# Layer 0 of a four-layer kernel: ScalarE takes over the output copies, and gathered rows are summed two tiles per three quads

## The reference, cut to what matters

```python
scores = softmax(flat @ router_w.T + router_bias)
topk_scores, topk_idx = top_k(scores, 4)                 # 4 experts for each row
topk_scores = topk_scores / sum(topk_scores)
h = silu(flat @ gate_w[e].T) * (flat @ up_w[e].T)        # each expert e, hidden size 128
expert_out = h @ down_w[e].T
out = sum over the 4 chosen e of topk_scores[e] * expert_out[e]
out = out + silu(flat @ sgate_w.T) * (flat @ sup_w.T) @ sdown_w.T    # shared part
```

## Time and profile before

| | us |
|---|---|
| median of the runs | 1239.35 |
| the profiled execution, its own time | 1241.5 |
| its span in the trace | 1239.7 |
| the quad loop of layer 0, first `gate_up` to last output copy | 452.6 to 669.0 |
| first instruction of the RWKV phase | 672.17 |

### The profile page before, as it was taken

The page is one execution under the profiler, slowest core; times in us unless marked ns, Lnnn a source line. Parts: engine busy times, 40 slices in busy tenths (PEclk is TensorE's granted clock), DMA queues, the critical chain, the costliest instruction groups (busy, mean ns, idle before and its releaser), DMA issues. The chain is left out here.

```text
span 1239.7 us, 19813 instructions
## 1 busy us (share of the span) xinstructions
PE 897.0 (72%) x5652; PEld 691.5 (56%) x5652; DVE 783.5 (63%) x2423; ACT 630.2 (51%) x1304; POOL 513.5 (41%) x634
## 2 busy tenths in 40 slices
PE   3796666664439999929974466677668999999910
PEld 2633555553328889929863134344457977777710
DVE  5489589998765657404777699999867411016436
ACT  4355677774833234414322566776665545555500
POOL 0003555554146666644773775000005662036055
PEclk9998777776559999969987778888777999999965
DMA  7950000000501146436543111000031132223032
GB/s 208 289 160 1 1 0 0 0 0 20 222 28 44 45 128 191 142 121 176 159 125 100 47 47 31 1 0 1 1 130 53 57 107 82 61 75 96 27 94 60
DMA packets 133844, 97.00 MB, mean 78 GB/s; under 512 B 11648, under 2 KB 125696, under 8 KB 132736
## 3 DMA queue, kind: packets, MB, share of 16 engines
q1 hardware_dynamic: 121472, 70.79, 19.1%
q0 software_dynamic: 12288, 25.19, 6.9%
HBM read 45.61 MB, written 50.33 MB: 77 GB/s over the span
## 5 line engine op out<-in xcount | busy, mean ns | idle before, releaser
L1110 POOL DMA_INDIRECT e_xs<-h_tok,rows_of x128 | 128.8, 1007 | 101.7 <-DVEq L1571 35.4
L739 ACT ACTIVATE mask<-ps_q,k_neg 128x256 bf16<-128x256 f32 x256 | 101.0, 489 | 37.3 <-PE ps_q L853 37.3
L1123 POOL DMA_INDIRECT e_got<-e_ys,e_rows_of x64 | 65.7, 1027 | 127.1 <-DMA e_ys<-e_y_rows 108.2
L1259 PE MATMUL e_ps_gu<-e_w_all,e_x_turned 128*128 x384 | 96.9, 398 | 12.8 <-DVE e_hidden L1729 12.7
L1738 DVE COPY e_y_rows<-e_ps_y 128x512 f32<-128x512 f32 x20 | 13.8, 692 | 137.9 <-PE e_ps_y L1307 137.9
L853 PE MATMUL ps_q<-q_parts,pick 128*128 (+1 forms) x256 | 59.4, 368 | 48.9 <-DVE mask L651 42.1
L1442 ACT ACTIVATE e_hidden<-e_ps_up 128x512 f32<-128x512 f32 x80 | 47.8, 597 | 84.2 <-PE e_ps_up L1289 84.2
L2226 POOL DMA_INDIRECT c_got<-e_ys,rows_of x64 | 71.2, 1112 | 36.2 <-issue 19.2
L1110 POOL DMA_INDIRECT e_xs<-h_tok,e_rows_of x64 | 65.5, 1024 | 49.4 <-DVEq L1571 17.1
L1259 PEld LDWEIGHTS e_ps_gu<-e_w_all,e_x_turned 128*128 128x128 f32 x384 | 72.5, 199 | 23.0 <-issue 14.4
L1437 ACT ACTIVATE e_hidden<-e_ps_gu 128x512 f32<-128x512 f32 x48 | 28.7, 598 | 110.4 <-PE e_ps_gu L1259 110.4
(11 more groups left out here) (403 smaller groups left out, 2499.3 us busy)
## 6 DMA issues: line engine op xcount, KB each, us to landing
e_x_rows<-e_xs SPq DMA_DIRECT2D x68, 256.0 KB, 2.8
e_ys<-e_y_rows SPq DMA_DIRECT2D x68, 256.0 KB, 2.3
e_xs<-zeros SPq DMA_DIRECT2D x2, 6144.0 KB, 34.2
e_w_all<-in_w SPq DMA_DIRECT2D x4, 1536.0 KB, 13.5
e_xs<-zeros SPq DMA_DIRECT2D x2, 2560.0 KB, 27.4
e_w_all<-in_w SPq DMA_DIRECT2D x4, 1024.0 KB, 10.9
x_tok<-in_x SPq DMA_DIRECT2D x4, 512.0 KB, 6.2
e_xs<-h_tok,rows_of POOLq DMA_INDIRECT x128, 2.2
```

What stands on the lines that cost most here:

```text
L739: last = nc.scalar.activation(mask[u][QS // 2 + j][keys][:, h * T:(h + 1) * T], psq[1][:, h * T:(h + 1) * T], ACT.Sign, bias=k_neg[u][:, k ...
L1110: nc.gpsimd.indirect_dma_start(out=xs[part], out_offset=bass.IndirectOffsetOnAxis(ap=rows_of[:, t * K + k:t * K + k + 1], axis=0), in_=til ...
L1123: nc.gpsimd.indirect_dma_start(out=got[t % GB][:, k * P:(k + 1) * P], out_offset=None, in_=ys[part], in_offset=bass.IndirectOffsetOnAxis(a ...
L1259: last = nc.tensor.matmul(ps_gu[n % 2][:, t * 2 * P:(t + 1) * 2 * P], x_turned[n % 2][:, t * P:(t + 1) * P], at(w_all, col, 2 * P), start= ...
```

## The change

Three things change, all in layer 0's quad loop.

- `y_out` moves from VectorE to ScalarE, as the last thing in each of its steps. ScalarE's loop gets the steps 48 to 50, since the copy of quad n-3 is in step n.
- `combine_slot` gives tiles 2j and 2j+1 to the steps 31+3j and 32+3j, and none to the step 33+3j: two tiles per three quads. With 51 steps that places tiles 0 to 13. Tiles 14 and 15 are summed behind the loop (`late`).
- VectorE's two `advance(3)` around the copy become one `advance(6)`.

The second routed layer keeps its slots and its copies on VectorE.

```diff
             def combine_slot(n):
-                part, i = divmod(n, JQ if gated else JT)
-                i -= 6 if gated else 12
+                if gated:
+                    trio, i = divmod(n - JQ - 7, 3)
+                    return 2 * trio + i if trio >= 0 and i < 2 else None
+                part, i = divmod(n, JT)
+                i -= 12
                 return (part - 1) * PT + i if part and 0 <= i < PT else None
...
             (ScalarE)
+                def y_out(q):
+                    act.wait_ge(y_ps, FROM + q + 1)
+                    if q >= YB:
+                        act.wait_ge(stored[q % YB], FROM + 16 * (q // YB))
+                    nc.scalar.activation(y_rows[q % YB][:, :], bank_y(q)[:, :], ACT.Copy).then_inc(y_sb, 1)
...
-                    for n in range(QUADS + TURN_H):
+                    for n in range(QUADS + DOWN):
                         if n < QUADS:
                             silu_out(n)
-                        if n >= TURN_H:
+                        if 0 <= n - TURN_H < QUADS:
                             h_out(n - TURN_H)
                         if n + TURN_X < QUADS:
                             x_out(n + TURN_X)
+                        if n >= DOWN:
+                            y_out(n - DOWN)
...
             (VectorE)
-                        advance(3)
-                        if n >= DOWN:
-                            y_out(n - DOWN)
-                        advance(3)
+                        advance(6)
...
-                for t in range((NP - 1) * PT, OVER * PT):
+                late = [t for t in range(OVER * PT) if t not in map(combine_slot, range(steps))]
+                for t in late:
                     combine(t)
                     advance(None)
```

More of the change, by code:

```diff
@@ L1734, in y_out @@
                 def y_out(q):
-                    dve.wait_ge(y_ps, FROM + (q + 1) * (1 if gated else TPG))
+                    dve.wait_ge(y_ps, FROM + (q + 1) * TPG)
                     if q >= YB:
```

## The result

The changed kernel takes 1233.56 us (median of 5 runs, 1232.79 to 1234.71). The kernel before takes 1240.33 us (median of 5 runs on the same chip). The ratio is 0.9945, with a 95% interval of 0.9932 to 0.9959. 1233.0 us were forecast. Ratios in this document leave out executions that fell into a slower state of the chip and medians are of all executions, so two medians needn't divide to the ratio beside them. The profiled execution took 1234.71 us and its span is 1232.9, which is 6.8 less than the span before.

A forecast was written before the change was run, and what follows sets the result against it. POOL's gathers were taken to bound the kernel, through DVE. From tile 15's release at 657.5, DVE's chain ends at 665.3; 0.60 for the barrier gives 665.9 instead of 672.24, so 1239.35 - 6.3 = 1233.0 us, range 1230.5 to 1237.0.

The forecast's parts named there:

- Parts 1 and 2, the copy: Layer 0's loop: copies leaving DVE worth nothing by themselves; on ACT 0.60 us each, 1.1 us left before the SiLU.
- Part 3, the slots: Layer 0's loop: combines in the steps to 47 wait for nothing, so `gate_up(47)` comes at 636.8 us.
- Part 4, the end: End of layer 0's phase: DVE, bound to POOL, is last; next phase at 665.9 instead of 672.24, 6.3 us less.
- the gathers' start and pace: POOL's gathers in layer 0: start 0.09 us earlier, pace as before, plus or minus 0.5 us in all.
- The next phase's clock: PE behind the barrier: its longer idling costs 0, as the granted clock there is 0.60 already.
- Gathers later: Rival, 7%: evenly spread loads and stores cost each of 40 gathers 0.1 us more; 2.3 us gain left, 1237 us.
- PE's whole stall back: Rival, 2%: the end moves by all of the 18.7 us that stalls cost PE's loop, to 1220.7 us.
- ScalarE as the bound: Rival, 4%: after the restart at 550, ACT's copies wait for stores, delaying SiLU and gathers; slower, up to 1245.7 us.
- just under DVE's end: Barrier ending layer 0's phase: POOL's drain, started at 639.7, took 25.4 us to 665.1, against DVE's end at 665.3.

The follow-up runs named there:

- The doubled copy: Changed kernel with each of layer 0's 48 loop outputs copied twice on ScalarE, on another chip; PE's step 3.49 to 3.50 us, no total time given.
- chips A and B: Copy alone and slots alone, against the kernel before: 0.9951 and 1.0003 on chip A, 0.9982 and 0.9964 on chip B; whole change on chip B 0.9898.

## Why the prediction was right

The changed kernel came out 0.56 us from the forecast, by the mechanism that was forecast. Part of that closeness is luck. The gain was 6.8 us between the two medians, 0.5 more than the 6.3 of the forecast, and the median of the kernel before, by two more executions, came out at 1240.33 instead of the 1239.35 from which the forecast was reckoned. The two differences go against each other. Step by step:

**Parts 1 and 2, the copy.** Held: 0.60 us, 1.13 us left before the SiLU (1.1 was forecast). The gathers start 0.31 us earlier where 0.09 was forecast. The other 0.22 is PE's restart, 549.92 instead of 550.14. The doubled copy shows, where no gather runs, that PE's path has room for twice as much.

**Part 3, the slots.** Held on the first chip. `gate_up(47)` starts at 636.14, forecast 636.8. Of the 0.7 less, 0.25 is the earlier restart (556.18 instead of 556.43) and 0.44 the last step, where there is nothing to turn any more (3.06 us from 633.09 to 636.14, instead of 3.50). PE has no wait for a product, and DVE waits for gathers only behind step 47, for tiles 14 and 15. That it is the slots that end the loop early is shown by the traces of chips A and B. That they do it by moving the sums behind the gathers' landing is read from the first chip's two traces, not shown by an experiment: on the other chips gathers were early anyway.

**Part 4, the end.** The chain of terms came out nearly to the digit:

| | forecast | measured |
|---|---|---|
| last gather starts | 654.77 | 653.97 |
| to tile 15's release | 2.71 | 2.65 |
| release to the end of the statistics | 7.78 | 7.79 |
| to the next phase | 0.60 | 0.58 |
| next phase | 665.9 | 664.99 |

The one term that was off is the gathers' start and pace, put at 0.09 us in all. It gave 0.31 by the start and 0.58 by the interval (63 times 0.009). I had allowed plus or minus 0.5 for the pace and named what could free GpSimd. Which of the removed waits and copies did it, the runs don't tell. By the rule of the Trainium skill on a VectorE instruction with at most one SBUF input outside the two-port modes ("SBUF — State Buffer", Who interferes with whom), none of it would come from the copies. Chip B agrees, as far as it goes: there a gather takes 1.02 us on the mean with the copy on either engine. On the first chip it took 1.026 before and 1.018 after, and no run separates the causes of that.

The next phase's clock was put at nothing, and the granted clock there is 0.61 after 0.60. From the barrier on, 0.45 us of the 7.25 was given back, 0.11 in the RWKV phase and 0.34 in the last; that is within what executions scatter.

**The rivals.** Gathers later: no, they came earlier, at a DMA share of 0.57 instead of 0.47 in the stretch. PE's whole stall back: the last `gate_up` did come 19.4 us earlier, but the next phase only 7.25. The rest is idle time, and PE stands for 21.9 us from 643.1 to the barrier's end. On chip A leaving out gathers and their sums moved the barrier, so it is their row that PE stands for. ScalarE as the bound: refuted by PE's steps of 3.50 us and no wait of PE in the changed kernel, and the doubled copy agrees where no gather runs. The least certain sentence was the one on the drain "just under DVE's end". It was under by 0.23 us, and it turned out to be no accident of the trace but a fixed 9.2 us behind the last gather. Had the change cut DVE's end by more than about 0.5 us as well, a forecast by DVE's terms alone would have failed there.

## What to carry to other kernels

When a stall goes, ask what is last then, and add that chain term by term from rows, instead of counting the stall: here a loop's end 19.4 us earlier on TensorE was worth 7.25. A sum that waits for a transfer belongs where the transfer's own pace puts it, not one to every step. And a piece of work moved ahead of a wait is free only where the wait is really there, and only up to its length.

## What the runs showed of the hardware

GpSimd's drain at the end of a block costs 9.2 us behind its last indirect gather: 9.20 and 9.24 on the first chip, 9.2 on chip A, and 9.216 on chip B from the drain's begin, with every gather already landed. Without an indirect transfer in its block a drain took 0.81. Here it hid behind DVE's residual, whose end came 0.23 us later.

The same program needs 7 to 9% more time on three other chips. The steps of the loop are the same there to 0.01 us (3.50) while GpSimd is idle, and stall while it gathers. In places ACT then starts its instructions at even distances, as if each one came late by itself. Timeline of ACT in the changed kernel on chip B:

```profile
597.12 0.60 ACT L1440 ACTIVATE e_hidden<-e_ps_gu 128x512 f32<-128x512 f32 x1 [4.38 <-remote]
599.26 0.60 ACT L1450 ACTIVATE e_h_turned<-e_ps_ring 128x512 f32<-128x512 f32 x1 [1.54 <-remote]
601.39 0.60 ACT L1434 ACTIVATE e_x_turned<-e_ps_ring 128x512 f32<-128x512 f32 x1 [1.53 <-PE e_ps_ring L1250]
```

That is 2.13 us from one to the next, where 0.48 is usual. What holds them is open; the profile names no releaser that explains it.
